# An FFN with a convolution before it: W loaded from two DMA queues, and the prologue put in another order

## The reference

```
y   = conv1d(x, weight, 9 taps, 4 groups) + cond @ c_weight.T + bias_c     # 64 x 64 x 1024
b   = sample // 8                                # 8 groups of 8 samples, each with its own mix
A_b = sum_n gate[b,n] lora_A[n]  (32 x 1024);    B_b = sum_n gate[b,n] lora_B[n]  (1024 x 32)
out = x + y @ kernel + bias + (y @ A_b.T) @ B_b.T + (y @ A_s.T) @ B_s.T
```

## Time and profile before

| | us |
|---|---|
| median of 3 runs | 530.34 (529.39 to 531.42) |
| the profiled execution, its own time | 530.98 |
| its span, first to last instruction | 529.2 |
| prologue, to the last `lowrank` of the first half | 74.27 |
| last wait of PE on a load in it (`lb`) | ends at 46.48 |

### The profile page before, as it was taken

The page is one execution under the profiler, slowest core; times in us unless marked ns, Lnnn a source line. Parts: engine busy times, 40 slices in busy tenths (PEclk is TensorE's granted clock), DMA queues, the critical chain, the costliest instruction groups (busy, mean ns, idle before and its releaser), DMA issues.

```text
span 529.2 us, 6509 instructions
## 1 busy us (share of the span) xinstructions
PE 510.4 (96%) x2372; PEld 414.0 (78%) x2372; DVE 242.3 (46%) x302; ACT 144.8 (27%) x175; POOL 207.5 (39%) x124
## 2 busy tenths in 40 slices
PE   4699989999999999999999999999999999999996
PEld 3456778888888888888888888888888888888884
DVE  3878684446243552437243462328334363424311
ACT  2545514322313141221323133220324123131000
POOL 1576954542516053341615243261605334171100
PEclk9899999999999999999999999999999999999999
DMA  8995769441834256240934247240833313141212
GB/s 216 302 242 183 159 228 220 177 112 36 199 96 112 66 141 170 76 113 11 207 106 112 75 109 179 72 116 30 202 115 90 98 53 102 24 120 48 86 41 72
DMA packets 19575, 65.05 MB, mean 123 GB/s; under 512 B 3274, under 2 KB 3914, under 8 KB 18922
## 3 DMA queue, kind: packets, MB, share of 16 engines
q1 hardware_dynamic: 17690, 63.46, 45.0%
q10 hardware_dynamic: 1872, 1.41, 1.1%
HBM read 45.59 MB, written 18.87 MB: 122 GB/s over the span
## 4 chain that ended last, share of the span: by engine, by line
PE 90%; DMA 4%; DVE 2%; POOL 1%; issue 1%; ACTq 0%; ACT 0%; DVEq 0%
PE main L793 65%; PE conv L748 16%; PE rank L806 6%; PE main L798 3%; DMA lb<-in_L_ffn_lora_B 3%; DMA x_in<-in_x 1%; DVE x_tr L537 1%; PE conv L785 1%; POOL as_st L321 1%; ACT x_hi L413 0%; PE spare L761 0%; DVE w_raw L584 0%; POOL x_lo L313 0%; DVE res L665 0%; DVE y_lo L572 0%
## 5 line engine op out<-in xcount | busy, mean ns | idle before, releaser
L335 POOL TENSOR_TENSOR y_lo<-y_stage,y_hi 128x512 fp32r<-128x512 f32 x60 | 77.6, 1295 | 242.1 <-ACT y_hi L428 242.1
L793 PE MATMUL main<-w_hi,y_hi 128*128 128x512 f32 x512 | 160.1, 391 | 1.4 <-DVE res L665 1.4
L793 PE MATMUL main<-w_lo,y_hi 128*128 128x512 f32 x512 | 159.5, 390 | 0.0
L793 PE MATMUL main<-w_hi,y_lo 128*128 128x512 f32 x512 | 159.4, 390 | 0.0
L793 PEld LDWEIGHTS main<-w_hi,y_hi 128*128 128x128 f32 x512 | 96.0, 188 | 22.4 <-issue 1.8
L793 PEld LDWEIGHTS main<-w_lo,y_hi 128*128 128x128 f32 x512 | 96.1, 188 | 20.9
L793 PEld LDWEIGHTS main<-w_hi,y_lo 128*128 128x128 f32 x512 | 96.1, 188 | 20.6
L428 ACT ACTIVATE y_hi<-y_stage 128x512 fp32r<-128x512 f32 x64 | 40.5, 632 | 236.5 <-DVE y_stage L566 236.5
L556 DVE TENSOR_TENSOR y_add<-conv,ctx_all 128x512 f32<-128x512 f32 x64 | 44.2, 690 | 121.3 <-PE conv L748 120.8
L329 POOL TENSOR_TENSOR x_lo<-x_tr,x_hi 128x1032 fp32r<-128x1032 f32 x30 | 87.9, 2929 | 25.0 <-ACT x_hi L433 25.0
L566 DVE STREAM_TRANSPOSE y_stage<-y_add 128x512 f32<-128x512 f32 x64 | 75.6, 1181 | 6.6
(11 more groups left out here) (76 smaller groups left out, 286.9 us busy)
## 6 DMA issues: line engine op xcount, KB each, us to landing
res<-in_x SPq DMA_DIRECT2D x32, 512.0 KB
out<-res SPq DMA_DIRECT2D x31, 512.0 KB
x_in<-in_x SPq DMA_DIRECT2D x28, 512.0 KB, 11.1
w_raw<-in_L_ffn_kernel SPq DMA_DIRECT2D x16, 256.0 KB, 19.0
b_cur<-b_scratch SPq DMA_DIRECT2D x21, 128.0 KB, 2.4
la<-in_L_ffn_lora_A SPq DMA_DIRECT2D x4, 512.0 KB, 14.1
lb<-in_L_ffn_lora_B SPq DMA_DIRECT2D x1, 2048.0 KB, 14.5
b_scratch<-be_hi SPq DMA_DIRECT2D x4, 256.0 KB, 6.0
```

What stands on the lines that cost most here:

```text
L335: nc.gpsimd.tensor_tensor(y_part(y_lo, h, t, mh), y_stage[:, i % 2, :], y_part(y_hi, h, t, mh).bitcast(F32), ALU.subtract).then_inc(ylo_do ...
L793: mm(main[t][:, n * 512:(n + 1) * 512], lhs, rhs[:, k, n * 512:(n + 1) * 512], start=k == 0 and first, stop=False)
```

## The change

- W: each quarter is loaded half by SP (jh 0 and 1, partitions 0 to 63) and half by ACT (jh 2 and 3, partitions 64 to 127). ACT issues its halves between its computations. SP's queue now has `la` ahead of all of W.
- x: three of the four DMAs of x_first[0] stand first in SP's queue; all four of x_first[1] are issued by ACT after `bias_hi`, behind its half of quarter 0. The row of `x_in` becomes 1056 elements, and x begins 16 elements into it, instead of 1032 and 4.
- The convolution weights are loaded contiguously (`w_nat`) and spread by a DVE copy into `w_pad`. PE transposes them ahead of the conditions. `cw_rep` is made by ACT instead of DVE. The channel bias is no longer added by four matmuls with `ones` but in the copy to `ctx_all`, from a column `cbias` loaded by four DMAs of single elements to 128 partitions.
- The lists of PE and DVE get another order: `mix_a` ahead of the merges, `chunk(1)` ahead of the third convolution, `mix_b` later by one chunk and spread out, the second half of `x_turn` after `w_add(3)`. In the first chunk the products with `w_lo` come last. `convolve` takes `x_lo` last.

```diff
-        def load_w(eng, ma):
-            for jh in range(4):
+        def load_w(eng, ma, jhs):
+            for jh in jhs:
                 eng.dma_start(w_raw[jh * 32:(jh + 1) * 32, 2 * ma:2 * ma + 2, :].rearrange("m j d -> m (j d)"),
                               kern_v[ma, jh]).then_inc(kern_in[ma], 16)
...
-            sp.dma_start(cbias[:, :], cond_bias.rearrange("(a c) -> a c", a=1)).then_inc(cbias_in, 16)
+            load_first(sp, 0, (0, 1, 2))
             sp.dma_start(gate_nat[:, :], gate).then_inc(gate_in, 16)
-            load_first(sp, 0, (0, 1))
-            load_shared(sp, 0)
-            load_shared(sp, 1)
-            load_first(sp, 1, (0, 1))
+            with nc.allow_non_contiguous_dma(reason="small"):
+                for g in range(G):
+                    sp.dma_start(cbias[:, g:g + 1], bass.AP(cond_bias.tensor, cond_bias.offset + g * CG, [[0, J], [1, CG], [1, 1]])
+                                 ).then_inc(cbias_in, 16)
+            for q in range(3):
+                load_shared(sp, q)
...
-            load_w(sp, 0)
             for q in range(RQ):
                 sp.dma_start(la[:, q, :], la_v[:, q, :]).then_inc(la_in[q], 16)
-            for ma in range(1, 4):
-                load_w(sp, ma)
+            for ma in range(4):
+                load_w(sp, ma, (0, 1))
...
-            act.dma_start(w_pad[:, :, PAD:PAD + TAPS], conv_w).then_inc(cw_in, 16)
+            act.dma_start(w_nat[:, :], conv_w.rearrange("o c k -> o (c k)")).then_inc(cw_in, 16)
...
-            load_first(act, 0, (2, 3))
-            load_shared(act, 2)
-            load_first(act, 1, (2, 3))
-            act.wait_ge(cond_tr, 1)
-            nc.scalar.activation(cond_t[:, :], rank[:, 0:NS], ACT.Copy).then_inc(cond_cp, 1)
+            load_first(act, 0, (3,))
...
             nc.scalar.activation(bias_hi[:, :], bias_nat[:, :], ACT.Copy).then_inc(bias_split, 1)
+            load_w(act, 0, (2, 3))
+            load_first(act, 1, range(CH))
...
             y_high(0, 0, 1, FIRST)
+            load_w(act, 1, (2, 3))
             w_high(0)
             w_high(1)
+            load_w(act, 2, (2, 3))
+            load_w(act, 3, (2, 3))
             x_first_high(1)
...
-            w_add(0)
-            w_add(1)
-            y_first_low(0)
-            y_first_low(1)
-            dve.wait_ge(x_first[1], 64)
-            x_turn(0, 4)
-            a_turn(0)
-            x_turn(0, 5)
-            a_turn(1)
+            a_turn(0)
+            a_turn(1)
+            y_first_low(0)
+            y_first_low(1)
+            w_add(0)
+            w_add(1)
+            a_turn(2)
+            a_turn(3)
             w_add(2)
             w_add(3)
-            x_turn(0, 6)
-            x_turn(0, 7)
-            a_turn(2)
-            a_turn(3)
+            dve.wait_ge(x_first[1], 64)
+            for c in range(XH, XC):
+                x_turn(0, c)
...
+            mix_a(0)
+            mix_a(1)
             merge(0)
             merge(1)
-            mix_a(0)
-            mix_a(1)
+            mix_a(2)
+            mix_a(3)
             merge(2)
             merge(3)
...
-            chunk(0, (0,))
+            pe.wait_ge(y0_lo, 2)
+            pe.wait_ge(whi_done, 1)
+            dense(0, 0, 0, products=(0, 2))
             pe.wait_ge(a_done, RQ)
-            chunk(0, (1,))
+            dense(0, 1, 0, products=(0, 2))
+            pe.wait_ge(wlo_done, 1)
+            for t in range(2):
+                dense(0, t, 0, products=(1,))
+            merge(4)
+            merge(5)
+            chunk(1)
             convolve(0, 0, 2, FIRST, first=True)
             merge(6)
             merge(7)
-            chunk(1)
+            chunk(2)
             convolve(0, 0, 3, FIRST, first=True)
             merge(8)
             merge(9)
-            chunk(2)
+            chunk(3)
             mix_b(0)
-            mix_b(1)
             merge(10)
             merge(11)
-            chunk(3)
-            mix_b(2)
-            mix_b(3)
+            mix_b(1)
             merge(12)
             merge(13)
             chunk(4)
+            mix_b(2)
+            mix_b(3)
             merge(14)
             merge(15)
             pe.wait_ge(b_turned, RQ)
```

More of the change, by code:

```diff
@@ L28 @@
 PAD = J - 1
+EDGE = 16
+ROW = EDGE + L + EDGE
 WIN = 2 * J
@@ L90, in adaln_ffn @@
         lb, = early(("lb", [P, 2, 2048], F32))
-        x_in = sb("x_in", [P, CL, L + 2 * HALO])
+        x_in = sb("x_in", [P, CL, ROW])
         x_tr = sb("x_tr", [P, MB, SB, G])
@@ L95, in adaln_ffn @@
         y_add, y_stage = sb("y_add", [P, 2, 512]), sb("y_stage", [P, 2, 512])
-        (w_pad, cond_nat, cw_nat, cond_t, cw_rep, cbias, bias_rep, ones, gate_nat, gate_rep, diag) = early(
-            ("w_pad", [C, CG, PAD + TAPS + PAD], F32), ("cond_nat", [NS, CD], F32), ("cw_nat", [C, CD], F32),
-            ("cond_t", [CD, NS], F32), ("cw_rep", [P, G, J, CG], F32), ("cbias", [1, C], F32),
-            ("bias_rep", [1, G, J, CG], F32), ("ones", [1, NS], F32), ("gate_nat", [NB, NL], F32),
+        (w_pad, w_nat, cond_nat, cw_nat, cond_t, cw_rep, cbias, gate_nat, gate_rep, diag) = early(
+            ("w_pad", [C, CG, PAD + TAPS + PAD], F32), ("w_nat", [C, CG * TAPS], F32), ("cond_nat", [NS, CD], F32), ("cw_nat", [C, CD], F32),
+            ("cond_t", [CD, NS], F32), ("cw_rep", [P, G, J, CG], F32), ("cbias", [P, G], F32),
+            ("gate_nat", [NB, NL], F32),
             ("gate_rep", [NB, NL, R8], F32), ("diag", [P, R8], F32))
@@ L405, in _ @@
                                      ACT.Copy).then_inc(thi_done, 1)
+            act.wait_ge(cond_tr, 1)
+            nc.scalar.activation(cond_t[:, :], rank[:, 0:NS], ACT.Copy).then_inc(cond_cp, 1)
+            nc.scalar.activation(cw_rep[:, :, :, :], rank[:, NS:NS + C].rearrange("p (g c) -> p g c", g=G)
+                                 .unsqueeze(2).broadcast_to([P, G, J, CG]), ACT.Copy).then_inc(cwrep_done, 1)
             act.wait_ge(gate_in, 16)
@@ L641, in _ @@
             b_turn(0)
-            b_turn(1)
             w_add(10)
             w_add(11)
+            b_turn(1)
+            w_add(12)
+            w_add(13)
             b_turn(2)
             b_turn(3)
-            nc.vector.memset(x_in[:, :, 0:HALO], 0.0).then_inc(halo_zero, 1)
-            nc.vector.memset(x_in[:, :, HALO + L:], 0.0).then_inc(halo_zero, 1)
-            for m in range(12, 16):
+            nc.vector.memset(x_in[:, :, EDGE - HALO:EDGE], 0.0).then_inc(halo_zero, 1)
+            nc.vector.memset(x_in[:, :, EDGE + L:EDGE + L + HALO], 0.0).then_inc(halo_zero, 1)
+            for m in range(14, 16):
                 w_add(m)
@@ L719, in _ @@
                 last.then_inc(t_tr, 1)
+            pe.wait_ge(cond_in, 32)
+            nc.tensor.transpose(rank[:, 0:NS], cond_nat[:, :], ident[0:NS, 0:NS])
+            nc.tensor.transpose(rank[:, NS:NS + C], cw_nat[:, :], ident[0:C, 0:C]).then_inc(cond_tr, 1)
             pe.wait_ge(cond_cp, 1)
             pe.wait_ge(cwrep_done, 1)
-            pe.wait_ge(biasrep_done, 2)
             for g in range(G):
                 cols = rank[:, 256 + g * NS:256 + (g + 1) * NS]
-                mm(cols, cw_rep[:, g, :, :].rearrange("p j c -> p (j c)"), cond_t[:, :], start=True, stop=False)
-                last = mm(cols, bias_rep[:, g, :, :].rearrange("a j c -> a (j c)"), ones[:, :], start=False, stop=True)
+                last = mm(cols, cw_rep[:, g, :, :].rearrange("p j c -> p (j c)"), cond_t[:, :], start=True, stop=True)
             last.then_inc(ctx_mm, 1)
@@ L739, in convolve @@
                 n = 0
-                for lhs, rhs in ((t_hi, x_hi), (t_hi, x_lo), (t_lo, x_hi)):
+                for lhs, rhs in ((t_hi, x_hi), (t_lo, x_hi), (t_hi, x_lo)):
                     if first and rhs is x_lo:
@@ L787, in mix_b, with dense @@
                 last.then_inc(b_mm, 1)
-            def dense(h, t, k, halves=(0, 1)):
+            def dense(h, t, k, halves=(0, 1), products=(0, 1, 2)):
                 yh, yl = y_hi[h][:, t, k, :], y_lo[h][:, t, k, :]
-                for lhs, rhs, first in ((yh, w_hi, True), (yh, w_lo, False), (yl, w_hi, False)):
+                for i in products:
+                    lhs, rhs, first = ((yh, w_hi, True), (yh, w_lo, False), (yl, w_hi, False))[i]
                     for n in halves:
@@ L816, in _ @@
             convolve(0, 0, 1, FIRST, first=True)
+            mix_a(0)
+            mix_a(1)
             merge(0)
             merge(1)
-            mix_a(0)
-            mix_a(1)
+            mix_a(2)
+            mix_a(3)
             merge(2)
             merge(3)
-            mix_a(2)
-            mix_a(3)
-            merge(4)
-            merge(5)
             def chunk(k, tiles=(0, 1)):
```

35 lines of the change are left out of this document (14 added, 21 removed).

## The result

| | before | after |
|---|---|---|
| median, us | 530.44 (529.39 to 531.42, 4 runs) | 541.44 (539.95 to 542.18, 4 runs) |
| ratio | | 1.0204, 95% interval 1.0175 to 1.0233 |
| span of the profiled execution | 529.2 | 540.3 |
| start of the first `finish`, which follows the first half's first `lowrank` | 74.29 | 84.74 |
| end of the first half's last `lowrank` | 74.26 | 86.57 |

The account below looks back on a forecast made before the run. PE's own pace bounds the loop, taken as unchanged; the prologue's end moves from 74.27 to 73.1, start and closed-hole gains mostly given back to three holes. That -1.1 us takes the median from 530.34 to 529.2, range 526.4 to 533.5.

Parts of the forecast that it names:

- Start: First loads of x: with three DMAs first on SP, x lands at 8.2 us instead of 11.3, a gain of 3.1.
- The holes behind `w_low`: PE in the prologue idles before chunks 1, 2 and 3: 1.9, 2.8 and 1.1 us, giving back most gains.
- ACT's issues: Six DMA issues before `y_high(0)` take 3.2 us, hidden but for 0.1; four later ones also come before x is there.
- `mix_b` found `lb` in place: Last part of the prologue: lb is in by 41, `mix_b(0)` wants it at 46.9, so no wait; bound 46.4.
- The sum of 529.2: Whole kernel: the prologue ends at 73.1 instead of 74.27, so the median goes from 530.34 to 529.2 us.
- Quarter 0 of W: Prologue load, halves on two queues: landed at 21.6 us, wanted by `w_add(0)` at 22.7.
- The second half of x: x_first[1] on ACT's queue behind W, taking equal shares: landed at 28.6 us, bounds 26.4 and 31.5.
- Conditions: Prologue: the four `cbias` DMAs of single elements delay the shared pair by up to 1.5 us, with 0.6 of cover.
- Rival 4: Two partition halves don't overlap, all at 229 GB/s: quarter 0 lands at 23.9, x_first[1] at 32.9; 533 us, chance 0.08.
- Rival 3: x_first[1] loses to W and lands at 31.5, chunk 3 ends 2.8 us later: 532.0 us, chance 0.12.
- Rival 2: PE's clock falls in the new holes: 532.5 us, 534 with the hole before chunk 1; chance 0.20.
- The rule that was weighed: Skill's rule that disjoint-half transfers serialize, giving 533 us; the forecast instead trusted a trace of 369 GB/s against 229.

Follow-up runs that it names:

- w_one_queue: The changed kernel with all of W in SP's queue and x_first[1] left on ACT's: 546.38 us, ratio 1.0295.
- bias_row_w0_then_x: The changed kernel with the bias as one row, and la, quarter 0, x_first[1], quarters 1 to 3 all in SP's queue: 531.38 us, ratio 1.0004.
- bias_row: The changed kernel with the bias loaded as one row of 64 elements, spread on chip, no single-element transfers: 535.74 us, ratio 1.0085.
- x_early: The changed kernel with x_first[1] issued early, two DMAs on each queue, ahead of la: 536.76 us, ratio 1.0124.

## Why the prediction was wrong

**The steps that held.** x_turn at 8.32 (*Start*, 8.2). The holes behind `w_low` as the cost of the order: 1.60 + 0.95 + 1.99 where the loads are in time, against 1.9 + 2.8 + 1.1; right in kind and nearly in sum, not one by one. ACT's issues stayed hidden. `mix_b` found `lb` in place, since everything was late. The sum of 529.2 for this schedule lies 2.2 us under the 531.38 of the kernel that has it (1.4 if each is taken against its own median of the kernel before: -1.1 forecast, +0.3 measured, interval -0.9 to +1.3). That it comes so near is in part luck: the prologue ended 2.0 us later than summed, 1.8 of it chunk 3 at half clock, and a wait of 1.37 us for DVE behind the first half, which the sum left where it was, had gone.

**The step that failed** is *Quarter 0 of W*: "SP's half runs 17.0 to 19.4, ACT's 18.3 to 20.7 on the other partitions; landed at 21.6". It landed at 31.0. Three assumptions were in it. That the two queues add up: from 19 to 31 us they moved 165, 227 and 220 GB/s, and by themselves W's halves gain a tenth. That ACT's half moves when it is issued: issued from 17.5 us on, it moved nothing before 24. And, not even stated, that each quarter has the rate for itself: SP had issued its halves of all four quarters by 15.1 us, so 2.45 MB were moved from 19 to 31 us (the rest of `la`, and SP's next quarters), while quarter 0 is 1.05 MB. Before, one queue kept the quarters in order. The kernels set the two causes apart. With the elements and two queues it landed at 31.0, without the elements at 27.1, and without the elements in one queue at 21.1, where the forecast had 21.6. The reading behind the first assumption was wrong too: "SP's queue is writing partitions 0 to 63 (quarter 0 of W)" from 11 to 14 us was x_first[1] on both queues up to 13 us.

**The second half of x** (28.6, bound 31.5; landed 40.0) failed with it. Equal shares of the two queues were near here: from 29 to 34 us ACT's queue moved 0.42 MB of x beside SP's 0.57 (in w_one_queue it was 1 to 3.4). But x stands behind ACT's half of quarter 0, and that landed 9.4 us late.

**The term that was mis-sized** is *Conditions*: "up to 1.5 us" for the single elements with a cover of 0.6. The wait for the shared pair was 1.8 us, near it. But the term left out SP's 2.67 us of issuing, and asked only for the next load in the queue, and the delay goes through the whole queue: `la`, forecast all in by 18, landed at 23.3 (16.5 without the elements), and it is 3.85 us at quarter 0 and 5.7 in the kernel's time. Where x_first[1] stands in its place, taking them away is worth 1.5 us (ratios 1.0032 and 1.0004, with intervals that overlap, so not shown to be more than noise), though quarter 0 and x come 3.7 us earlier without them: PE then waits longer behind `w_low` and runs chunk 3 mostly at half clock (4.5 us against 2.97).

**How the loss adds up**, by the medians' ratios, each against the kernel before on its own chip (10.8 us in all): without the elements 1.0085, so they are 6.3 us; with quarter 0 and x in one queue as well 1.0004, so the two unordered queues are 4.3; 0.2 is left. In the other order the parts are 9.1 and 1.5 us: each fault hides part of the other, and neither number belongs to one edit alone.

**The rivals.** Rival 4 had the right mechanism and too small a price (533, at 0.08): it counted one rate for both queues but let quarter 0 go first. Rival 3 was right that x loses to W, as w_one_queue shows (44.1 instead of 31.5), and nearly right in its shares. Rival 2 came too: the clock of 0.50 after the holes makes chunk 2 take 5.40 us instead of 2.77, and in bias_row_w0_then_x chunk 3 about 4.5. There no load is late, so that part belongs to the order's own holes. Each was priced as the only thing that goes wrong, though in the changed kernel all three have one cause, a late load, and the range was made from single cases. (Their chances for "slower" add up to 0.18, not 0.19.)

**The rule that was weighed.** The forecast said "the trace disagrees for 32-partition transfers". The runs side with the Trainium skill (DMA: Bandwidth & Descriptors, Rules for kernel authors): two transfers to disjoint halves of the partitions are not worth it. For W it is 19.0 against 21.2 us, for x 9.9 against 12.2, a tenth and a fifth and not half. The row of 369 GB/s was true and was of other transfers.

**What stays open.** Why one more queue helps x more than it helps W; why ACT's queue moves nothing at first after its issue while SP's is full (17.5 to 24 us, 17 to 23 in w_one_queue, 15.8 to 22 in bias_row, but only 19.0 to 22 in x_early); and why the issues behind the single elements are held up. The other row length of `x_in` and the order of the products in the first chunk were never changed alone. The start with x first has no run without the elements in before's order of work.

## What to carry to other kernels

A second DMA queue added a tenth or a fifth to the rate here, not a second rate, and it takes away an order: loads that are wanted one after the other belong in one queue in the order in which they are wanted, and a rate seen with one kind of transfer is measured again before another kind is moved on the strength of it. When a load stream is the bound, a delay early in a queue is to be followed to the last load that something waits for, not to the next one; a few hundred single elements cost more there than the bytes say. Rivals that hang on the same late load should be added up, not priced one by one. And a marker for the end of a stage should be what the next stage really waits for: here DVE's first `finish`, and not the last matmul, ended it in the kernel before.
